# Folding weight rows four deep and forming the low-rank product between the first matmuls of the third GEMM

## The reference, cut to what matters

```
x = x + tanh(g_xattn[0]) * attention0(layernorm(x), ctx)    # Wq, Wk, Wv, Wo: 1024 x 1024; 16 heads x 4 planes
x = x + tanh(g_ffn[0])   * ffn0(layernorm(x))
x = x + tanh(g_xattn[1]) * attention1(layernorm(x), ctx)    # windowed over the feature axis
x = x + tanh(g_ffn[1])   * ffn1(layernorm(x))               # clusters select rows and tokens

attention0: q, k, v = projection of the input, then  y + 0.1 * amp * (y mixed over the 4 planes of a head)
ffn0:       x @ W.T + bias + sum over 16 experts of  coeff*scale * (x @ A.T) @ Bf.T     # 16 experts of rank 16
```

## Time and profile before

| what | value |
|---|---|
| runs | 2161.71, 2163.52, 2165.14 us; median 2163.52 us |
| profiled execution | 2168.02 us, its span 2166.2 us |
| mean granted TensorE clock | 0.954 of full |
| TensorE busy | 1981.0 us, 91% |
| VectorE busy | 1069.4 us, 49% |
| ScalarE busy | 657.9 us, 30% |
| GpSimd busy | 372.4 us, 17% |
| read and written in HBM | 200.25 MB and 125.83 MB |

### The profile page before, as it was taken

One profiled execution on the slowest core, in us unless ns is written; L12 is line 12 of the kernel. 1 busy time (PEld: TensorE's weight loads), 2 busy tenths in 40 slices (PEclk: granted clock), 3 DMA queues, 4 the chain that ended last, 5 costly groups with the idle time before them and its releaser, 6 DMA issues. The chain is left out here.

```text
span 2166.2 us, 50916 instructions
## 1 busy us (share of the span) xinstructions
PE 1981.0 (91%) x20126; PEld 1601.4 (74%) x20126; DVE 1069.4 (49%) x1866; ACT 657.9 (30%) x1114; POOL 372.4 (17%) x342
## 2 busy tenths in 40 slices
PE   6999689999995999999998699999599999986998
PEld 6999689999994777777776277777367667764887
DVE  5444141112112555555553555554678787854443
ACT  2222131111100344434443111121267566652000
POOL 0000000000003411110110000000356555640000
PEclk9999899999996899999999799999799999996999
DMA  4332443434238544554441535554765454423432
GB/s 150 117 116 98 160 132 125 179 129 144 96 120 316 194 174 187 214 212 178 179 181 41 181 121 185 189 181 148 198 164 157 123 154 125 125 80 119 143 145 89
DMA packets 149429, 328.60 MB, mean 152 GB/s; under 512 B 56432, under 2 KB 82672, under 8 KB 141104
## 3 DMA queue, kind: packets, MB, share of 16 engines
q1 hardware_dynamic: 147344, 326.04, 42.8%
q10 hardware_dynamic: 1952, 0.60, 0.1%
HBM read 200.25 MB, written 125.83 MB: 151 GB/s over the span
## 5 line engine op out<-in xcount | busy, mean ns | idle before, releaser
L1506 ACT ACTIVATE a_pt<-a_st_bank 128x1024 f32<-128x1024 f32 x128 | 131.2, 1025 | 268.2 <-PE a_st_bank L1552 268.2
L1056 POOL TENSOR_TENSOR a_sm<-a_sm,a_nmax 113x1024 f32<-113x1024 f32 x84 | 159.6, 1907 | 93.9 <-DVE a_nmax L1109 93.9
L1458 DVE TENSOR_REDUCE a_nmax<-a_s_bank 128x8 f32<-128x1024 f32 x128 | 156.6, 1224 | 28.0 <-PE a_s_bank L1540 21.7
L268 PE MATMUL q_qb<-q_xt_hi,wq_hi 128*128 128x256 f32 x512 | 146.2, 286 | 3.0 <-DVE wq_lo L179 3.0
L268 PE MATMUL kv_kb<-kv_ct_hi,wk_hi 128*128 128x256 f32 x512 | 146.2, 286 | 3.0 <-DVE wv_lo L179 3.0
L268 PE MATMUL kv_kb<-kv_ct_lo,wk_hi 128*128 128x256 f32 x512 | 146.1, 285 | 0.0
L268 PE MATMUL kv_kb<-kv_ct_hi,wk_lo 128*128 128x256 f32 x512 | 146.1, 285 | 0.0
L268 PE MATMUL q_qb<-q_xt_hi,wq_lo 128*128 128x256 f32 x512 | 145.6, 284 | 0.0
L268 PE MATMUL q_qb<-q_xt_lo,wq_hi 128*128 128x256 f32 x512 | 145.5, 284 | 0.0
L1234 PE MATMUL a_s_bank<-a_ks,a_qs 64*49 64x256 f32 x1344 | 97.5, 404 | 33.0 <-DMA a_ks<-k 14.0
L1103 DVE TENSOR_TENSOR a_sm<-a_s_bank,a_band 113x1024 f32<-113x1024 f32 x84 | 102.7, 1223 | 28.0 <-PE a_s_bank L1234 25.8
(11 more groups left out here) (205 smaller groups left out, 4525.6 us busy)
## 6 DMA issues: line engine op xcount, KB each, us to landing
a_qs<-q SPq DMA_DIRECT2D x32, 1024.0 KB, 5.3
a_ks<-k SPq DMA_DIRECT2D x32, 1024.0 KB, 7.1
k<-kv_raw SPq DMA_DIRECT2D x32, 512.0 KB, 4.6
f_xin<-x SPq DMA_DIRECT2D x32, 512.0 KB, 4.3
a_vraw<-v SPq DMA_DIRECT2D x32, 304.0 KB
q_xin<-in_x SPq DMA_DIRECT2D x16, 512.0 KB, 5.6
q<-q_out_lo SPq DMA_DIRECT2D x16, 512.0 KB, 3.6
q<-q_out_hi SPq DMA_DIRECT2D x16, 512.0 KB, 4.3
```

The source lines that it names most:

```text
L268: m = pe.matmul(out, a(x, c), b(y, c), start=(i + j == 0), stop=(len(terms) * j + i == n - 1))
L1056: pool.tensor_tensor(sm[live, k], sm[live, k], nmax[live, k, :].unsqueeze(2).to_broadcast([LIVE, 16, KEYS]), ALU.add).then_inc(shifted, 1)
L1458: dve.tensor_reduce(to, s_bank[:].rearrange("p b (h x) -> p b h x", h=4), X, ALU.max, negate=True).then_inc(maxed, 1)
L1506: act.activation(pt[:, s % 2], st_bank[:].rearrange("p b (h x) -> p (b h) x", h=4), ACT.Exp).then_inc(expd, 1)
```

## The change

1. `FoldedWeight` loses its loops. It gets a list of bank pairs, and a row may be folded when the row as many before it as there are pairs has its `lo`. Wq and Wk get four pairs, Wv two. Loads wait on `folded` only from the fifth row on (Wv: from the third, with two buffers), so the first four need no signal.
2. project_q: the four pairs are the two of the product and the two of the transposes; before the third row TensorE waits until both transposed tiles have been read.
3. project_kv: SyncE loads four rows of Wk ahead of the context; TensorE folds Wk, and folds one row of Wv after each key block of group 0. `ready` of Wv stands ahead of the first value block. The split of the context of group 0 stands between the rows 3 and 4 of Wk on ScalarE and VectorE. Group 0 is written out ahead of the loop, group 7 behind it.
4. The low-rank factors get memory of their own, are loaded in attention0 by SyncE behind the load of x of the last batch, and are scaled by VectorE behind the `output` of the last batch but one.
5. ffn0_project1: SyncE loads x of tile 0 first, then two raw rows, the bias, two rows, x of tile 1 and four rows; there are eight raw buffers and no wait. TensorE forms the products of rows 0 and 1 at once, and those of rows 2 to 7 each ahead of the matmuls of chunk c = 0 to 5 of the first half of tile 0. Each chunk waits for its own row's `lo`. The `lo` is formed on GpSimd. On VectorE the first tile is normalised, then rows 0 and 1 are added, then the tile's `lo` is formed, row 2 is added, tile 1 normalised, and rows 3 to 7 added. The wait for `scaled` moves from the opening to each projection.

```diff
-    def fold(self, pe, banks):
...
-                pe.wait_ge(self.lo_done, free(self.base + RAW * i + k))
...
+    def load(self, sp, r):
+        slots = self.raw.shape[1]
+        if r >= slots:
+            sp.wait_ge(self.folded, r - slots + 1)
+        sp.dma_start(self.raw[:, r % slots, :], self.rows[r]).then_inc(self.loaded[r % slots], 16)
+
+    def fold(self, pe, r):
+        slots, depth = self.raw.shape[1], len(self.banks)
+        pe.wait_ge(self.loaded[r % slots], 16 * (r // slots + 1))
+        if r >= depth:
+            pe.wait_ge(self.lo_done, r - depth + 1)
...
@@ LowRankWeight
+    def product(self, pe, r):
+        if r > 1:
+            pe.wait_ge(self.summed, r - 1)
+        for h in range(2):
+            for n in range(2):
+                m = pe.matmul(self.banks[:, 2 * (r % 2) + h, :], self.e.lr_a[:, n, r * P:(r + 1) * P],
+                              self.e.lr_b[:, n, h * 512:(h + 1) * 512], start=n == 0, stop=n == 1)
+        m.then_inc(self.lr, 1)
+
+    def add(self, dve, r):
+        row = self.raw[:, r, :].rearrange("p (a b) -> p a b", a=2)
+        dve.wait_ge(self.loaded[r], 16)
+        dve.wait_ge(self.lr, r + 1)
+        dve.tensor_tensor(row, self.banks[:, 2 * (r % 2):2 * (r % 2) + 2, :], row, ALU.add).then_inc(self.summed, 1)
+
+    def split_lo(self, pool, r):
+        pool.wait_ge(self.hi_done, r + 1)
+        pool.tensor_tensor(self.lo[:, r, :], self.raw[:, r, :], self.hi[:, r, :].bitcast(F32),
+                           ALU.subtract).then_inc(self.lo_done, 1)
@@ project_q, TensorE
             def weights():
                 pe.wait_ge(biased, 1)
-                w.fold(pe, qb)
+                for r in range(NC):
+                    if r == 2:
+                        pe.wait_ge(xlo, done(1))
+                    w.fold(pe, r)
                 w.ready(pe)
@@ project_kv, SyncE
+            for r in range(RAW):
+                wk.load(sp, r)
             load(0, 0, 0)
-            wk.load(sp)
-            wv.load(sp)
+            for r in range(RAW, NC):
+                wk.load(sp, r)
+            sp.wait_ge(wk.folded, NC)
+            for r in range(NC):
+                wv.load(sp, r)
@@ project_kv, TensorE
-            wk.fold(pe, kb)
-            wv.fold(pe, kb)
-            wv.ready(pe)
+            for r in range(NC):
+                wk.fold(pe, r)
+            wk.ready(pe)
...
+            pe.wait_ge(clo, done(0))
+            for o in range(NC):
+                keys(0, 0, o)
+                wv.fold(pe, o)
+            wv.ready(pe)
+            values(0, 0)
+            with pe.Fori(0, (G - 2) // 2) as i:
+                product(2 * i + 1, 1)
+                product(2 * i + 2, 0)
+            product(G - 1, 1)
@@ ffn0_project1, SyncE
-            w.load_lowrank(sp)
...
-            sp.dma_start(biasb[:], e.i["bf0"].partition_broadcast(P)).then_inc(bias_in, 16)
             load_x(0, 0, 0)
+            for r in range(2):
+                w.load(sp, r)
+            sp.dma_start(biasb[:], e.i["bf0"].partition_broadcast(P)).then_inc(bias_in, 16)
+            for r in range(2, RAW):
+                w.load(sp, r)
             load_x(1, 1, 0)
-            weights()
+            for r in range(RAW, NC):
+                w.load(sp, r)
@@ ffn0_project1, GpSimd
+            root(0, 0, 0)
+            for r in range(3):
+                w.split_lo(pool, r)
+            root(1, 1, 0)
+            for r in range(3, NC):
+                w.split_lo(pool, r)
+            root(2, 2, 0)
@@ ffn0_project1, VectorE
             normalise(0, 0, 0)
+            w.add(dve, 0)
+            w.add(dve, 1)
+            turned_lo(0, 0, 0)
+            w.add(dve, 2)
             normalise(1, 1, 0)
-            weights()
+            for r in range(3, NC):
+                w.add(dve, r)
@@ ffn0_project1, TensorE
+                    opening = isinstance(t, int) and t + h == 0
+                    for c in range(NC):
+                        if opening and c + 2 < NC:
+                            w.product(pe, c + 2)
+                        if opening:
+                            w.ready(pe, c)
+                        for x, y in ((0, 0), (0, 1), (1, 0)):
+                            m = pe.matmul(gb[:, h, :], xt[x][:, s % 2, c, :], (w.hi, w.lo)[y][:, c, h * 512:h * 512 + 512],
+                                          start=c == x == y == 0, stop=c == NC - 1 and x == 1)
@@ attention0, VectorE, in output(u)
+                if isinstance(u, int) and u == N - NU - 1:
+                    dve.wait_ge(lr_in, 64)
+                    dve.tensor_tensor(ce[:, 2, :], ce[:, 0, :], ce[:, 1, :], ALU.mult).then_inc(lr_scaled, 1)
+                    dve.wait_ge(lr_scaled, 1)
+                    for n in range(2):
+                        dve.tensor_scalar(e.lr_b[:, n, :], e.lr_b[:, n, :], ce[:, 2, n:n + 1], None, ALU.mult)
```

More of the change, by code:

```diff
@@ L97, in begin, with __init__ @@
         eng.sem_inc(s, START)
[L100 to L111, removed]
 class FoldedWeight:
-    def __init__(self, nc, ctx, e, name, src, scale=1.0, share=None, raw=None):
+    def __init__(self, nc, ctx, e, name, src, raw, banks, scale=1.0):
         sb, ps, sem = scope(nc, ctx)
-        self.e, self.src, self.scale = e, src, scale
+        self.e, self.rows, self.scale = e, src.rearrange("(o p) c -> o p c", p=P), scale
         self.hi = sb(f"{name}_hi", [P, NC, D], F32R)
         self.lo = sb(f"{name}_lo", [P, NC, D], F32R)
[L124 to L130, removed]
+        self.raw, self.banks = raw, banks
+        self.loaded = [sem(f"{name}_loaded{k}") for k in range(raw.shape[1])]
         self.folded = sem(f"{name}_folded")
@@ new lines, in fold @@
+    def fold(self, pe, r):
[4 more added lines that the diff above has]
+        for c in range(NC):
+            m = pe.matmul(self.banks[r % depth][:, c // 4, c % 4 * P:(c % 4 + 1) * P],
+                          self.raw[:, r % slots, c * P:(c + 1) * P], self.e.fold[:, r, :], start=True, stop=True,
+                          skip_group_check=True)
+        m.then_inc(self.folded, 1)
@@ L528, in project_kv, with others @@
         ctx_t = e.i["ctxT"].rearrange("(c p) t -> p c t", p=P)
+        def others(eng, inputs, outputs):
+            with eng.Fori(0, (G - 2) // 2) as i:
+                for g in (1, 2):
+                    inputs(2 * i + g + 1, 1 - g % 2)
+                    outputs(2 * i + g, g % 2)
+            outputs(G - 1, 1)
         by_batch = lambda a: a.rearrange("p (b t) -> p b t", b=2)
@@ L625, in product @@
                                      range(NC)).then_inc(vmm, 1)
-            with pe.Fori(0, G // 2) as i:
-                for s in range(2):
-                    product(2 * i + s, s)
+            def product(g, s):
+                pe.wait_ge(clo, done(g))
+                for o in range(NC):
+                    keys(g, s, o)
+                values(g, s)
+            pe.wait_ge(clo, done(0))
+            for o in range(NC):
+                keys(0, 0, o)
[6 more added lines that the diff above has]
+            product(G - 1, 1)
 def staggered(eng, units, per_loop, stages, between=None, at=0, started=(), opening=None):
@@ L1763, in program @@
             project_kv(nc, e)
-        attention0(nc, e)
-        ffn0_project1(nc, e)
+        with ExitStack() as factors:
+            sb, ps, sem = scope(nc, factors)
+            e.lr_a = sb("f0_lr_a", [P, 2, D]); e.lr_b = sb("f0_lr_b", [P, 2, D])
+            attention0(nc, e)
+            ffn0_project1(nc, e)
         attend1_select_ffn1(nc, e)
```

256 lines of the change are left out of this document (115 added, 141 removed).

## The result

| | before | changed |
|---|---|---|
| runs beside each other | 2162.61 us (2159.28 to 2165.14, 4 runs) | 2137.71 us (2136.79 to 2140.18, 4 runs) |
| ratio, 95% interval | | 0.9881 [0.9860, 0.9903] |
| profiled execution, span | 2168.02, 2166.2 us | 2138.30, 2136.4 us |
| mean granted TensorE clock | 0.954 | 0.958 |
| TensorE busy | 1981.0 us | 1973.0 us |

The kernel became 24.9 us faster; 25.3 were forecast. The two profiled executions differ by 29.7 us, which is too much: the one before lay some 5 us above the median of all its runs. A second profiled execution of the unchanged kernel (experiment 5) took 2162.43 us, and stages are compared with both.

The account below looks back on a forecast made before the run. The kernel was taken as bound by TensorE's time plus its waits. Terms -7.0 - 5.7 - 13.5 + 0.9 = -25.3 us took the median from 2163.5 to 2138 us, range 2130 to 2149.

Parts of the forecast that it names:

- project_q (forecast -7.0): In project_q's opening, folded rows take 1.91 us each without waits, so products start at 38.2 instead of 45.2: -7.0 us.
- its upper end: In project_q, -8 us instead of -7.0 if the clock loss behind the wait ahead of the products shrinks too.
- project_kv (forecast -5.7): In project_kv, earlier folds and Wv folded between key blocks, less 2.3 us of clock for an added stop: -5.7 us.
- its end of -8.5: In project_kv, the favourable end of the forecast: no clock loss behind the stops and rows on time, -8.5 us.
- ffn0_project1 (forecast -13.5): In ffn0_project1's opening, TensorE's idle time shrinks while low-rank work stays; -15.5, then +2.0 for half clock: -13.5 us.
- zero slack: In ffn0_project1, add 3 ends at 1221.9, exactly when product 5 wants its bank; no stop at these values.
- attention0 (forecast +0.9): In attention0, VectorE's scaling of the factors delays `rows_lo`, and TensorE waits until 1168.65: +0.9 us, between 0 and 2.
- 1 (GpSimd's chain): In ffn0, slower `lo` or late bias stalls product 5, and chunks 3 to 7 follow GpSimd: 4 to 6 us; 10 in 100.
- 2 (loads): Weight reloads needing 5.5 us instead of 3.6 bound the folds; project_q and project_kv get 3 us less each: 2144; 9 in 100.
- 3: More than forecast: no clock loss behind the new stops (-4.3) and all upper ends, 2130 us; 7 in 100.
- 4: Interleaved stretches of project_kv's group 0 and ffn0 stay at half clock: slower, 2168 us or more; 2 in 100.
- 5: A wait in order binds TensorE to the old time in two of three stages: within 4 us of before; 3 in 100.

Follow-up runs that it names:

- experiment 1: The kernel before with the new project_q alone: 2163.13 us over 12 runs, ratio to before 0.9997.
- 2: The kernel before with the new project_kv alone: 2158.28 us over 8 runs, ratio to before 0.9971.
- experiment 10: The changed kernel with the low-rank products of rows 2 to 7 all ahead of chunk 0 in ffn0, none interleaved: 2135.39 us, ratio to before 0.9871.
- 7: The changed kernel with the values' weight folded a row ahead of its key block in project_kv: 2133.94 us, ratio to before 0.9865.
- experiment 3: The kernel before with the new ffn0_project1 and attention0's early loading of the factors: 2150.54 us, ratio to before 0.9939.
- experiment 11: The changed kernel with the `lo` of the ffn0 weight back on VectorE instead of GpSimd: 2135.74 us, ratio to before 0.9869.
- 7 to 12: Six variants of the changed kernel, with edits to the waits and folds of project_q and project_kv or to ffn0: 2119.87 to 2135.74 us.
- experiment 4: The changed kernel measured and profiled once more, nothing edited: 2136.21 us over 4 runs, ratio to before 0.9878.
- experiment 8: The changed kernel with products in project_q and project_kv waiting for five or six folded rows instead of eight: 2130.91 us, ratio to before 0.9847.
- the last version: The changed kernel with values' weight folded ahead, products waiting for fewer rows, and low-rank rows moved earlier in ffn0: 2119.87 us, ratio to before 0.9793.
- 6: The changed kernel with the old project_q put back, all else new: 2146.85 us over 5 runs, ratio to before 0.9917.

## Why the prediction was right

The forecast time holds, 24.9 us against 25.3, and so does the reading of the stops: which went, which came and who ends them. Single terms do not hold as well; they cancel, as is told at the end.

**project_q (forecast -7.0).** The products started 6.6 us earlier than in the first profile (5.9 than in the second, 44.5), over the table's executions the stage lost 8.2. A row of the fold takes 3.57 / 2 = 1.79 us and not 1.91: the 2.05 us that I divided was that of rows behind a wait, and in a line the same row is 1.95 long. The reloads did not have 2 us to spare: the last was 0.8 us late. These two terms cancel. About 2 of the 8.2 us are clock, which the forecast had as its upper end: in the first 60 us each profile with the old part had one or two stretches of 3.4 us at the lower clock, of the table's three with the new part only experiment 1 had one. What I did not see is that 1.2 to 1.8 us come back at once, in the way to the first fold.

**project_kv (forecast -5.7).** The piece shrank by 9.6 us (with the old q part 419.5, the mean of three, to 409.9, of two), 4 more than forecast, but the time by 6.3 when it was alone: in that profile the unchanged attention1 took 4 us more than in the other rows with the old kernel's stages. The first fold came 14.2 us behind the last product of project_q, not 12.8: SyncE's first issue came 0.4 us later behind that product, and the load landed 4.5 us after its issue (244.99 to 249.50), where I had taken 3.5. With the old project_q ahead the forecast was exact: 12.86 us, and 3.6 from issue (252.75) to the first fold (256.35). In exchange the first two rows took 5.0 us after the rest (249.50 to 254.51) and not 6.2, and the others 1.79 each: eight took 15.90 us, 17.7 were counted. VectorE's order is as forecast, its chain from the first fold to the last `lo` 18.8 us instead of 20.7. In the changed kernel the new stop and its price were there: 2.94 and 2.50 us, each with the lower clock behind it. Other executions with the same stops didn't pay it (2 and 10 behind both, 7 behind the first), which the forecast had as its end of -8.5. The Trainium skill (TensorE: Matmul & The Clock Gate, "HAM oscillation — how this bites in real kernels") says so of waits between bursts, and in these two places the changed kernel's trace agrees; behind the stop of project_q it does not, nor do the traces of the executions just named.

**ffn0_project1 (forecast -13.5).** Measured -13.2, both as time (experiment 3) and as length of the piece (340.7 to 327.5). TensorE waited 5.22 us for tile 0 (4.9 forecast). VectorE waited 1.58 us for the bias, which was there 8.5 us behind the stage's first load (1173.41 to 1181.91; 7.6 forecast). A chunk took 4.13 us (4.1), the stop before chunk 7 3.16 (3.5). At product 5 zero slack was forecast: it cost 0.4 us (the chunk that follows starts at 1207.53; at the pace of the others, 3.03 behind 1204.07, it would be 1207.10). The idle times sum to 6.2 + 5.2 + 3.2 + 0.4 = 15.0 us against 14.3.

**attention0 (forecast +0.9).** The scaling did push `rows_lo`, and TensorE waited 0.37 us for it. The whole stage was not longer, 505.7 and 505.4 us against 506.3 and 506.1.

```profile
1149.16 0.41 PE L1608 MATMUL a_b_bank<-ident_sb,a_osb 128*128 128x128 f32 x2 [0.37 <-DVE wo_xt_lo L1483]
```

**The rivals.** 1 (GpSimd's chain) fell: the eight `lo` took 2.34 to 2.38 us each, and experiment 11 without it is no faster. Whether GpSimd and VectorE hold each other back did not come up: the changed kernel's L767 (L766 before) ran from 1201.52 to 1202.80, and GpSimd was idle from 1200.64 to 1205.11. 2 (loads) fell but for 0.8 us in project_q and the first load of project_kv. 3 did not come in the time; the missing clock loss that it was built on did, in single executions. 4 and 5 fell.

**Where it was right by luck.** The sum holds to 1 us, the single terms do not. By the lengths of the pieces, with both new parts against both old, project_q gave 8.2 us (7.0 forecast), project_kv with the way into it 7.5 (418.2 to 421.6, mean 419.5, against 412.0; 5.7 forecast), ffn0 13.2 (13.5), attention0 0.6 (a loss of 0.9). That is some 4 us more than the forecast, and attention1, which had no term, takes 2 of them back: it lies at 433.1 to 434.3 us in the four profiles with the old project_kv and at 435.3 to 440.6 in nine of the ten with the new (7 to 12: 435.3 to 436.1), the tenth being the 431.1 of experiment 4. Its granted clock goes with its length (0.93 at 431.1, 0.91 at 440.6, from the last of ffn0 to the last of attention1). So this is not mere chance between executions, as eight profiles let one think, and why an unchanged stage should follow project_kv is open. The ends of the forecast, too, were not added up as they stand: they give -13.5 and -33.5, where -17 to -32 was written; the result is far from both.

The products between the chunks, which give the change half its name, bring nothing (experiment 10). What is left for the gain in ffn0 is the factors loaded a stage ahead and the opening that works on the weight and on tile 0 at once. No run takes these two apart; by the idle times the first is 9.9 of 12.9 us (16.09 to 6.20, of 27.9 to 15.0).

Left open is why the same wait costs the lower clock in one execution and not in the other, and so why the q part is worth nothing alone and 8 us with the others. Where its gain went alone is known in size: 1.8 us are the longer way to the first fold, and 4.8 us are the estimate from the mean clock of the runs. That the lower clock is caused by the q part, and is not two sets of runs that fell out differently, isn't shown.

## What to carry to other kernels

Read an opening as a list of stops of TensorE, each with who ended it, and price a stop with what the clock costs behind it: here the last version has some 11 us less of idle time than the changed kernel (3.3 in project_q, 4.6 in project_kv, 3.5 in ffn0) and is 19 us faster. That price is no constant: behind the same stop it was nothing or 1.7 us, about half and half. Ask of each wait if it is for all that was prepared or only for what the next instruction reads; `ready` for eight rows, in two stages, cost 7 us (experiment 8, 0.9847 against 0.9880) where the first five would do. And measure a part both alone and as the one left out: the two can differ, here by 7 us, with an interval of some 5 to either side. Last, look at what follows a changed stage, too: the way into the next one grew by 1.2 to 1.8 us, in every profile.

## What the runs showed of the hardware that was not expected

- The same wait of 2.81 us was followed by 0.41 us records in one execution and by 0.28 us records in another of the same code. Over three such stops of 2.5 to 2.9 us and all profiles, 14 of 23 were followed by the lower clock.
- An unchanged stage, attention1, took from 431.1 to 440.6 us in the eight executions of the table; ffn0 in those with the same code stayed within 0.7 us. Over all fourteen it was longer with the new project_kv, but for one.
- Half a megabyte as the first load of project_kv, with three more and the context behind it, was used 3.6 and 3.7 us after issue with the old project_q ahead (2, 6) and 4.4 to 4.6 us with the new, where two packets of the `instruction` queue lie beside it.
- Folds of four rows in a line start 1.79 us apart, 8 x 2 records of 128x128; the timeline's merged rows show 1.95 for one row and 3.74 for two.
